# Up-projection as seven block products of 256 tokens instead of eight, with its weights combined during attention and streamed from DRAM

## What is computed

```
for l in range(2):
    x = x + local_attention(shift_token(x), wqkv[l], ...) @ wo[l]
    h = layernorm(shift_token(x)) * ln_g[l] + ln_b[l]       # 4096 x 512
    a, g = split(h @ w1[l] + b1[l])                         # the up-projection: 512 -> 2 x 1365
    x = x + (a * gelu(g)) @ w2[l] + b2[l]                   # the down-projection: 1365 -> 512
```

## Time and profile before

| | |
|---|---|
| time, median of 3 runs | 2969.84 us (2969.80 to 2969.89) |
| span of the profiled execution (first to last instruction) | 2968.6 us |
| what lies around the span (median less span) | 1.2 us |
| granted TensorE clock | 1.00 of full in every stretch |
| the two feed-forward parts | from about 853 and from about 2235 us on |

### The profile page before, as it was taken

One profiled execution on the slowest core, in us unless ns is written; L12 is line 12 of the kernel. 1 busy time (PEld: TensorE's weight loads), 2 busy tenths in 40 slices (PEclk: granted clock), 3 DMA queues, 4 the chain that ended last, 5 costly groups with the idle time before them and its releaser, 6 DMA issues. The chain is left out here.

```text
span 2968.6 us, 44295 instructions
## 1 busy us (share of the span) xinstructions
PE 2948.6 (99%) x17064; PEld 2417.8 (81%) x17064; DVE 1621.6 (55%) x3367; ACT 1228.2 (41%) x2501; POOL 1151.9 (39%) x1190
## 2 busy tenths in 40 slices
PE   9999999999999999999999999999999999999999
PEld 7887888888878888888887888888878888888887
DVE  8976767766664333333425767776775333333331
ACT  7875555555563111111124555555565211111111
POOL 7856666665621110111113556656651111221111
PEclk9999999999999999999999999999999999999999
DMA  6751111111151011100121111111133111111110
GB/s 220 235 186 45 34 51 54 44 44 54 33 158 39 20 40 45 46 31 21 40 96 60 44 43 44 58 47 33 54 93 100 58 45 46 40 59 56 48 49 25
DMA packets 143189, 188.43 MB, mean 63 GB/s; under 512 B 21366, under 2 KB 75130, under 8 KB 142980
## 3 DMA queue, kind: packets, MB, share of 16 engines
q1 hardware_dynamic: 142836, 185.54, 19.5%
q10 hardware_dynamic: 144, 0.07, 0.0%
HBM read 130.34 MB, written 52.46 MB: 62 GB/s over the span
## 5 line engine op out<-in xcount | busy, mean ns | idle before, releaser
L1071 PE MATMUL quad<-fhT_f,w_h_f 128*128 128x512 f32 (+1 forms) x1392 | 550.8, 396 | 0.0
L1073 PE MATMUL quad<-fhT_f,w_l_f 128*128 128x512 f32 (+1 forms) x1392 | 544.9, 391 | 0.0
L1072 PE MATMUL quad<-fhT_f,w_h_f 128*128 128x512 f32 (+1 forms) x1392 | 543.4, 390 | 0.0
L1780 DVE SCALAR_TENSOR_TENSOR u_f<-quad,bias_f,gate_f_raw 128x512 f32<-128x512 f32 (+1 forms) x174 | 130.4, 749 | 705.2 <-PE quad L1073 621.9
L1853 POOL TENSOR_SCALAR stats<-stats 128x1 f32<-128x1 f32 x64 | 43.4, 678 | 1017.1 <-DVE stats L1755 1016.4
L1303 ACT ACTIVATE lprob<-lprob,small 128x384 f32<-128x384 f32 (+2 forms) x512 | 288.6, 565 | 159.4 <-DVE small L1623 159.4
L1947 POOL TENSOR_TENSOR turned_qk<-with_cos,with_sin 128x256 f32<-128x256 f32 x252 | 181.0, 739 | 442.5 <-DVE with_sin L1647 386.4
L1409 ACT ACTIVATE gate_f_raw<-quad,bias_f 128x512 f32<-128x512 f32 (+1 forms) x174 | 119.5, 687 | 512.0 <-PE quad L1073 512.0
L1135 ACT ACTIVATE uT_f<-u_f 128x512 fp32r<-128x512 f32 (+2 forms) x176 | 117.3, 666 | 503.7 <-DVE u_f L1780 503.7
L828 PE MATMUL bank_pair<-wqkv_h,hT 128*128 128x512 f32 x992 | 318.9, 402 | 0.0
L1073 PEld LDWEIGHTS quad<-fhT_f,w_l_f 128*128 128x128 f32 (+1 forms) x1392 | 256.8, 184 | 63.1
(11 more groups left out here) (236 smaller groups left out, 6047.9 us busy)
## 6 DMA issues: line engine op xcount, KB each, us to landing
s_in<-stream SPq DMA_DIRECT2D x128, 128.0 KB, 2.7
s_res<-stream SPq DMA_DIRECT2D x64, 256.0 KB, 2.9
stream<-a_out SPq DMA_DIRECT2D x64, 256.0 KB, 2.0
w_h_f_raw<-in_L_ffn_w SPq DMA_DIRECT2D x60, 256.0 KB, 5.2
h_in_f<-stream SPq DMA_DIRECT2D x112, 128.0 KB, 2.5
res_f<-stream SPq DMA_DIRECT2D x47, 256.0 KB, 3.1
x_in<-in_x SPq DMA_DIRECT2D x32, 256.0 KB, 3.0
x_dram<-x_out SPq DMA_DIRECT2D x32, 256.0 KB, 2.4
```

The costliest lines, as they stand in the source:

```text
L1071: e.matmul(bank[0:n, :], high, hT[:, 0, c, :], start=c == 0, stop=False)
L1072: e.matmul(bank[0:n, :], high, hT[:, 1, c, :], start=False, stop=False)
L1073: ins = e.matmul(bank[0:n, :], low, hT[:, 0, c, :], start=False, stop=c == KC - 1)
L1780: e.scalar_tensor_tensor(out=Fm.u[q % 2][0:n, :], in0=up_bank(2 * (g * HC + j) + 1)[0:n, :], scalar=Fm.bias1[0:n, 0, j:j + 1], in1=Fm.gate ...
```

## The change

- **Products.** Rows of a group are paired (tiles 0 and 2 against 1 and 3, 256 tokens each), and the up-projection of a block is done by seven products of half the inputs and half the tokens (Strassen's scheme in Winograd's form), each 2 chunks x 3 matmuls of 256 columns: 42 matmuls of 256 columns in place of 24 of 512. They go to four banks (`product_banks`), by `up_first`, `up_second` and `up_third`.
- **Sums behind them.** ScalarE's `keep_first` copies the first product (256 columns); VectorE adds (`add_first`, `add_second` 512 columns each, `add_third` 512 and 256). `gate` and `make_u` then read SBUF.
- **Rows.** Per group, high and low of 7 combinations of the rows are kept. For groups 1 to 7 `keep_turned` copies the transposes, GpSimd makes four combinations per pair of tiles (`sum_rows`), ScalarE and VectorE split them (`split_rows`). For group 0 seven units are turned from rows kept in DRAM (`turn_unit`, 28 transposes in place of 16).
- **Weights.** In steps 2 to 26 of attention, every second step, SyncE loads one block of w1 (three DMAs of 512 B rows), GpSimd makes four sums of 256 columns (`sum_parts`) in the next step, ScalarE rounds (`round_sums` 1024, `round_parts` 768 columns), VectorE makes the rests (`split_sums` 1024, `split_parts` 768), and four DMAs store them (1.835 MB a block). In the feed-forward part every block's 14336 B x 128 partitions are streamed into one of three slots (`load_slot`), two to three blocks ahead, for each group anew. Only w2 stays in SBUF (`down_split`).

The core of the diff, with what stands in the attention loops and the block loop of the feed-forward part:

```diff
+def prepared_item(s, after):
+
+    item, odd = divmod(s - PREPARE_AT - after, 2)
+    return item if 0 <= item < HC and not odd else None
...
+        def load_parts(l, j):
+            n = hid_rows(j)
+            w1v = w1[l].rearrange("(c p) n -> p c n", p=P)
+
+            def unit(at, units):
+                return raw_sum[:, at * 2 * n:(at + units) * 2 * n].rearrange("p (c n) -> p c n", n=n)
+
+            w.wait_ge(S("parts_out"), 64 * (l * HC + j))
+            load(unit(0, 1), w1v[:, 0:2, HID + j * P:HID + j * P + n], S("parts_in"))
+            load(unit(1, 2), w1v[:, :, j * P:j * P + n], S("parts_in"))
+            load(unit(3, 1), w1v[:, 2:KC, HID + j * P:HID + j * P + n], S("parts_in"))
+
+        def store_parts(l, j, sums):
+            n, to = hid_rows(j), parts_dram[l][j]
+            w.wait_ge(S("part_low"), 2 * (l * HC + j) + (1 if sums else 2))
+            if sums:
+                load(to[:, 0, 6 * n:], part_high[:, 0:8 * n].bitcast(F32), S("parts_out"))
+                load(to[:, 1, 6 * n:], part_low[:, 0:8 * n].bitcast(F32), S("parts_out"))
+            else:
+                load(to[:, 0, 0:6 * n], part_high[:, 0:6 * n].bitcast(F32), S("parts_out"))
+                load(to[:, 1, 0:6 * n], raw_part[:, 2 * n:8 * n].bitcast(F32), S("parts_out"))
+
+        def load_rows_to_mix(l, pair):
+            w.wait_ge(S("parts_out"), 64 * (l + 1) * HC)
...
+                    if p == 0 and prepared_item(s, 2) is not None:
+                        store_parts(l, prepared_item(s, 2), False)
...
+                    if p == 1 and prepared_item(s, 0) is not None:
+                        load_parts(l, prepared_item(s, 0))
...
+                    if p == 2 and prepared_item(s, 1) is not None:
+                        store_parts(l, prepared_item(s, 1), True)
...
+        def load_slot(l, k):
+            i, j = k % 3, k % HC
+            if k >= 3:
+                w.wait_ge(S("products"), 4 * (l * BLOCKS + k - 2))
+            load(ffns[l].slots[i][:, 0:4 * UNITS * hid_rows(j)].bitcast(F32),
+                 parts_dram[l][j].rearrange("p h n -> p (h n)"), S("slot_in", i))
...
+            def sum_parts(j):
+
+                n = 2 * hid_rows(j)
+                g1, a1, a2, g2 = (raw_sum[:, i * n:(i + 1) * n] for i in range(4))
+                s1, s2, s3, s4 = (part_sum[:, i * n:(i + 1) * n] for i in range(4))
+                w.wait_ge(S("parts_in"), 48 * (l * (HC + 2) + j + 1))
+                settle(combine(ALU.add, s1, g1, g2))
+                combine(ALU.subtract, s3, a1, g1)
+                settle(combine(ALU.subtract, s2, s1, a1))
+                combine(ALU.subtract, s4, a2, s2).then_inc(S("part_sums"), 1)
...
+                if prepared_item(s, 1) is not None:
+                    sum_parts(prepared_item(s, 1))
...
-            for c in range(first, last):
-                high, low = w1_part(Fm.block_h[j], j, half, c), w1_part(Fm.block_l[j], j, half, c)
-                e.matmul(bank[0:n, :], high, hT[:, 0, c, :], start=c == 0, stop=False)
-                e.matmul(bank[0:n, :], high, hT[:, 1, c, :], start=False, stop=False)
-                ins = e.matmul(bank[0:n, :], low, hT[:, 0, c, :], start=False, stop=c == KC - 1)
...
+        def product(l, g, j, unit, combo, bank):
+            n, hT = hid_rows(j), ffns[l].hT[g % 2]
+            for c in (0, 1):
+                high, low = part(l, g, j, 0, unit, c), part(l, g, j, 1, unit, c)
+                row_high, row_low = hT[:, 0, 2 * combo + c, :], hT[:, 1, 2 * combo + c, :]
+                e.matmul(bank[0:n, :], high, row_high, start=c == 0, stop=False)
+                e.matmul(bank[0:n, :], high, row_low, start=False, stop=False)
+                ins = e.matmul(bank[0:n, :], low, row_high, start=False, stop=c == 1)
...
+        def up_first(l, g, j):
+
+            k, base = g * HC + j, l * TILES
+            q, (d, a, _) = l * BLOCKS + k, product_banks(g, j)
+            w.wait_ge(S("fhT_low"), turned_before(l, g + 1))
+            w.wait_ge(S("slot_in", k % 3), 16 * (slot_loads(l, k % 3) + k // 3 + 1))
+            if k == 1:
+                w.wait_ge(S("oT_low"), base + TILES)
+            elif k:
+                w.wait_ge(S("s1"), q)
+                turned_here = (TILES - GROUP) * l + GROUP * g + len([i for i in (2, 4, 6, 8) if i < j and g + 1 < GROUPS])
+                w.wait_ge(S("raw_in"), min(turned_here, (TILES - GROUP) * (l + 1)))
+            if l + 1 < DEPTH and k == BLOCKS - 1:
+                w.wait_ge(S("hT_low"), base + TILES + 1)
+            product(l, g, j, 0, 0, d[:, 0:HALF_ROWS]).then_inc(S("products"), 1)
+            if k == 1:
                 w.wait_ge(S("lprobT"), PAIRS * (base + TILES))
...
+            product(l, g, j, 0, 0, d[:, 0:HALF_ROWS]).then_inc(S("products"), 1)
+            if k == 1:
                 w.wait_ge(S("lprobT"), PAIRS * (base + TILES))
...
+            elif k:
+                w.wait_ge(S("up_sums"), 3 * q - 2)
+            product(l, g, j, 4, 4, a[:, HALF_ROWS:])
+            product(l, g, j, 1, 1, a[:, 0:HALF_ROWS]).then_inc(S("products"), 1)
+
...
+        def up_second(l, g, j):
+
+            k = g * HC + j
+            q, (_, _, bc) = l * BLOCKS + k, product_banks(g, j)
+            if k == 0:
+                w.wait_ge(S("up_sums"), 3 * q + 1)
+            elif k > 1:
+                w.wait_ge(S("up_sums"), 3 * q - 1)
+            product(l, g, j, 3, 3, bc[:, 1, 0:HALF_ROWS])
+            product(l, g, j, 5, 5, bc[:, 1, HALF_ROWS:]).then_inc(S("products"), 1)
+
+        def up_third(l, g, j):
+
+            k = g * HC + j
+            q, (_, _, bc) = l * BLOCKS + k, product_banks(g, j)
+            if k == 0:
+                w.wait_ge(S("s1"), q + 1)
+            elif k > 1:
+                w.wait_ge(S("up_sums"), 3 * q)
+            product(l, g, j, 6, 2, bc[:, 0, 0:HALF_ROWS])
+            product(l, g, j, 2, 6, bc[:, 0, HALF_ROWS:]).then_inc(S("products"), 1)
 
         def ffn(l):
...
+        def add_first(l, g, j):
+
+            Fm, n, q = ffns[l], hid_rows(j), l * BLOCKS + g * HC + j
+            a, sums = product_banks(g, j)[1], Fm.sums[q % 2]
+            w.wait_ge(S("products"), 4 * q + 2)
+            w.wait_ge(S("s1"), q + 1)
+            e.tensor_tensor(sums[0:n, 0:4:2, :], a[0:n, :].rearrange("p (u n) -> p u n", u=2),
+                            Fm.first[q % 2][0:n, :].unsqueeze(1).to_broadcast([n, 2, HALF_ROWS]),
+                            ALU.add).then_inc(S("up_sums"), 1)
+
+        def add_second(l, g, j):
+
+            Fm, n, q = ffns[l], hid_rows(j), l * BLOCKS + g * HC + j
+            bc, sums = product_banks(g, j)[2], Fm.sums[q % 2]
+            w.wait_ge(S("products"), 4 * q + 3)
+            w.wait_ge(S("up_sums"), 3 * q + 1)
+            settle(e.tensor_tensor(sums[0:n, 1:4:2, :], bc[0:n, 1, :].rearrange("p (u n) -> p u n", u=2),
+                                   sums[0:n, 2, :].unsqueeze(1).to_broadcast([n, 2, HALF_ROWS]), ALU.add))
+
+        def add_third(l, g, j):
+
+            Fm, n, q = ffns[l], hid_rows(j), l * BLOCKS + g * HC + j
+            bc, sums = product_banks(g, j)[2], Fm.sums[q % 2]
+            w.wait_ge(S("products"), 4 * q + 4)
+            if (g, j) == (0, 0):
+                w.wait_ge(S("parts_out"), 64 * HC * (l + 1))
+                w.wait_ge(S("mixed_out"), 32 * (l + 1))
+            if g and j == 1:
+                w.wait_ge(S("stacked"), 32 * (l * GROUPS + g + 1))
+            e.tensor_tensor(Fm.gate[q % 2][0:n, :].rearrange("p (u n) -> p u n", u=2),
+                            flat(bc[0:n, :, :])[:, HALF_ROWS:3 * HALF_ROWS].rearrange("p (u n) -> p u n", u=2),
+                            sums[0:n, 3, :].unsqueeze(1).to_broadcast([n, 2, HALF_ROWS]), ALU.add).then_inc(S("up_sums"), 1)
+            e.tensor_tensor(sums[0:n, 1, :], bc[0:n, 0, 0:HALF_ROWS], sums[0:n, 1, :], ALU.add).then_inc(S("up_sums"), 1)
 
...
-                    for order in (0, 1):
-                        up(l, g, j, order)
-                    if j == 1:
+                    up_first(l, g, j)
+                    up_second(l, g, j)
+                    if g + 1 < GROUPS and j in (2, 4, 6, 8):
+                        w.wait_ge(S("s1"), step + g * HC + j + 1)
+                        turn_normalised(l, (g + 1) * GROUP + j // 2 - 1)
+                    if l + 1 < DEPTH and (g, j) == (GROUPS - 1, 9):
+                        turn_first_rows(l + 1)
+                    up_third(l, g, j)
+                    if g and j == 1:
                         down(g - 1, FULL)
...
+                    if d == 0 and prepared_item(s, 2) is not None:
+                        split_parts(l, prepared_item(s, 2))
+                    if d == 0 and prepared_item(s, 1) is not None:
+                        split_sums(l, prepared_item(s, 1))
...
+                        add_first(l, g, j)
+                        add_second(l, g, j)
+                        if l + 1 < DEPTH and (g, j) == (GROUPS - 1, 9):
+                            split_first_rows(l + 1)
```

(10 more changed lines are left out.)

705 lines of the change are left out of this document (430 added, 275 removed).

## The result

2984.73 us (median of 4 runs, 2980.58 to 2987.41) against 2969.86 before: 1.0048 times the time, interval 1.0034 to 1.0062. The forecast was 2944, and faster; the changed kernel is 0.5% slower, 0.3 us inside the upper end of the range of 2890 to 2985. The profiled execution has a span of 2982.2 us, 13.6 above that of before.

The account below looks back on a forecast made before the run. TensorE's own work was taken to bound the kernel. 2968.6 - 88 + 2.6 + 2 + 33 + 13 + 12 = 2943.2, plus 1.2 around the span, gave 2944 us; range 2890 to 2985.

Parts of the forecast that it names:

- products, 16 groups: Feed-forward up-projection: 42 matmuls of 256 columns for 24 of 512 gain 0.50 us a block, 88 us over 176 blocks.
- early tiles, waits: Attention steps with an early-stored tile: weights land late, GpSimd's rotation slips, TensorE waits; 16.4 us a layer, +33 us.
- attention otherwise, its tail, turned units of group 0: VectorE delays in every attention step +13 us, last steps losing filler matmuls +2, extra transposes for group 0 +2.6.
- VectorE's bursts: Feed-forward: VectorE's normalisations and splits pile up within a group, 0.9 us for each of 14 groups, +12 us.
- at the full granted clock: Opening step on what bounds the kernel: TensorE busy in 99% of the span, at full clock, so time is its work.
- DMA.** ... I take 0: Feed-forward weight stream: 19.6 MB a group, 262 GB/s with existing traffic, loads issued some 18 us ahead; cost 0.
- a place on VectorE with little slack in odd steps: Attention, between the splits of hT and oT: odd steps delayed 0.5 us, 1.0 us with GpSimd's hold.
- Rival 2: Waits in both parts at upper bounds through holds by GpSimd's port: 2991 at most, 2970 in the middle; chance 0.14.
- the rule of the Trainium skill that the prediction cites: VectorE operations on two SBUF inputs lock the port shared with GpSimd throughout; by it the every-step attention term nears 30 us.
- Rival 1: Attention: weight loads land in time and GpSimd's 6 us of idle time hides all the work: 2895; chance 0.18.
- Rivals 3 to 5: Feed-forward: VectorE bounds it, 3043, chance 0.07; streaming bounds it, 3216, 0.03; 256-column matmuls at 0.109 us, 2870, 0.03.
- rival 4: Feed-forward: streaming bounds it below 262 GB/s; at 218, 103 us a group, 3216 us; chance 0.03.

Follow-up runs that it names:

- experiment 2: Changed kernel with useless repeated matmuls of the v projection filling TensorE's wait in steps 13, 15, 17 and 19, loads still late: 2973.69 us.
- experiment 1: Changed kernel with SyncE's early store, and its wait, moved behind the stores and load of weight blocks: 2932.73 us.
- experiment 9: Changed kernel with early store and sums' split later, turning behind last products, weight loads halved around stacking DMAs: 2907.51 us; then without the weight stream: 2900.98.
- experiment 8: Against the kernel with stacking DMAs on ScalarE's queue (3000.13 us), each 43-row stacking DMA issued as 32 and 11 rows: 2973.2 us.
- experiment 10: Changed kernel with early store and sums' split later, turning behind last products, 43-row stacking DMAs as 32 and 11 rows on SyncE's queue: 2902.84 us.
- e12: The kernel of experiment 8: stacking DMAs on ScalarE's queue, the 43-row ones issued as 32 and 11 rows: 2973.2 us.
- e1: The kernel of experiment 1: changed kernel with the early store behind the weight blocks' stores and load: 2932.73 us.
- e2: The kernel of experiment 2: changed kernel with useless matmuls filling TensorE's wait in four attention steps a layer: 2973.69 us.
- e6: On top of e1, SyncE issues the stacking DMAs ahead of the next 1.8 MB load of weights: 2937.98 us.

## Why the prediction was wrong

Terms of its sum against what was measured, in us (spans; a group is the distance from one group's first adding of its result to the next one's):

| term | forecast | measured | from |
|---|---|---|---|
| products, 16 groups | -88 | -81 | steady group 91.65 before; 87.54 - 0.95 after |
| early tiles, waits | +33 | +37.1 | wait list |
| attention otherwise, its tail, turned units of group 0 | +13 +2 +2.6 | +15.1 | attention parts 59.4 longer, less 37.1 and 15.7; group 0 behind them 2.2 longer, plus 10.1 (its products), less 3.8 (four bursts) |
| VectorE's bursts | +12 | +13.3 | 14 x 0.95 |
| clock behind the waits | 0 | +21.0 | 15.7 + 5.3 |
| stacking DMAs | 0 | +8.0 | wait list |
| sum | -25.4 | +13.5 | spans: +13.6 |

The third row is what is left over ("behind them" is from a layer's last mixing to the first product of group 1, 87.0 us in both layers before, 87.7 and 88.5 after), so that the sum closes says little of it. Part of it is work moved: 24 matmuls of 512 columns stood ahead of the last mixing of a layer, and now 18 of 256.

**The steps that failed.** First, "So 3 x 3.8 + 5 = 16.4 us a layer, **+33 us**": the chain, its lateness and the wait are right to 12%, but a wait was priced at its own length. Each of these also drops the clock, which adds 16 us here and 5 in the feed-forward parts; experiment 2 shows TensorE's standing still as the cause, experiment 1 that both go together. The forecast reads "at the full granted clock" off a kernel whose longest wait from 225 us on is 0.6 us. Second, "**DMA.** ... I take 0": right for the stream itself (experiment 9), wrong for what shares its engines. The stacking DMAs were not changed, so they were in no part of the change, but the queue ahead of them was: 8.0 us, settled by experiment 8, where only the rows of the DMA changed, and seen again in experiment 10 on SyncE's queue. (With their clock they cost 11.0 us: `e12`, without them, has the feed-forward parts 4.8 and 6.2 us shorter. That is less than 8.0 + 5.3, because two of the turning's waits hide behind them.) These two are 29 of the 39 us between the forecast span and the measured one; the products 7, the early tiles 4.

**The products** gave 5.06 us a group, not 5.5. The 0.229 us for 512 columns holds in the runs of `up` before; the mis-sized term is 0.119 for 256 columns, where the products stand 0.1198 apart from the first to the last of a run of 42. A block gains 24 x 0.229 - 42 x 0.1198 = 0.46 us, 11 blocks 5.1. The formula that the prediction takes from the Trainium skill stands there for a single matmul in isolation; the page has 131 ns for 512 columns in a stream, and no distance here is that short.

**Right**: the place, cause and size of the eight waits; the size of VectorE's bursts (0.95 against 0.9 a group, though seen by the turning and not by block 2); a place on VectorE with little slack in odd steps (0.35 to 0.5 us in each by the distance, not 1.0); the stream itself at no cost.

**The rivals.** Rival 2 gives the range in which the time fell, 2970 to 2991, and for the wrong reason: its holds by GpSimd's port didn't come. The two splits took 1.23 and 0.95 us at the median, 1.22 and 0.96 having been estimated, and TensorE's waits for the maxima, which the port was to raise to 30 us, are 5.8 in the list. Holds there are all the same, and the operation that began first isn't the one held. VectorE's split of the sums mostly begins first, and then it is GpSimd that is held (2.11 us for a scaling of probabilities that takes 1.24 alone); in 4 of 22 cases the other split begins inside a multiplication of GpSimd, and takes 1.47 to 1.51 us:

```profile
283.66 1.23 DVE L1713 TENSOR_TENSOR part_low<-part_low_raw,part_high 128x1024 fp32r<-128x1024 f32 x1 [0.25 <-ACT part_high L1349]
283.89 2.11 POOL L2271 TENSOR_SCALAR lprob<-lprob,small 128x384 f32<-128x384 f32 x1
...
566.87 1.04 POOL L2291 TENSOR_TENSOR turned_qk<-turned_qk,norm 128x512 f32<-128x512 f32 x1
567.25 1.48 DVE L1713 TENSOR_TENSOR raw_part<-raw_part_raw,part_high 128x768 fp32r<-128x768 f32 x1
```

For these operations the trace agrees with the rule of the Trainium skill that the prediction cites; the prediction's error was to let GpSimd always come first. GpSimd's long `norm<-norm,half_power` (3.1 us on 16 columns) holds nothing: splits that begin inside it take 0.95 us.

Rival 1's mechanism needed one moved store: with it (`e1`) 2933, and not its 2895. It left out the stacking DMAs (8.9), their clock (3.9) and the products' 7 us, and took the bursts at 6 us for 13.3; most of the rest lies in the table's third row. Rivals 3 to 5 fall: VectorE is busy in 68% of the steady part, the stream runs at 258 GB/s (the 218 that rival 4 reckons with stands in no row), the distance is 0.1198.

**Open**: how the table's third row divides; and why a DMA wait of 3.2 us in layer 0 of `e2` left the clock up while one of 1.9 us that ended at 501.28 did not.

## What to carry to other kernels

In a kernel whose TensorE never stops, price a new wait of some microseconds at its length and about half of the work behind it that runs at the low clock; and look in program order, on the issuing queue, at what stands ahead of each new load, since one early store behind a semaphore cost 52 us here. When a stream is put on DMA engines that were nearly idle, go through every small transfer that already had a deadline: its row count decides over how many engines it goes, and 43 rows as 32 and 11 were worth more than a queue of their own, which made it worse.

## What the hardware showed unexpectedly

- The granted clock at half for 3.4 to 13.7 us behind every wait of TensorE of 3.5 us and more; behind waits of 1.8 to 3.3 us sometimes (1.94 at 957.88 in `e6`) and sometimes not (1.91 at 2325.04 in `e6`, 3.24 in `e2`); not behind the waits under 1.3 us that every version has by the dozen.
- Two queues on one DMA engine take turns packet by packet: 2 KB packets 0.62 us apart beside packets of 14 KB, 0.165 us beside packets of 2 KB.
- A DMA of 43 rows in which one packet follows another, as on a single engine; 32 and 11 rows, all through in 2.6 us.
- A VectorE operation on two SBUF inputs and a scaling or multiplication of GpSimd hold each other, and mostly the one that began first runs at its own length: a split of 0.95 us takes 1.48 behind GpSimd, a scaling of 1.24 us takes 2.11 behind VectorE. GpSimd's `norm<-norm,half_power` of 3.1 us holds no split.
